# Attention maxima: one row block in eight found from a difference of scores

## The reference

```
keys = x @ jnp.triu(Wk).T
queries = x @ jnp.tril(Wq).T
values = x @ Wv.T
...
dot = jnp.einsum('bqhs,bkhs->bhqk', queries, keys) * scale
att = jax.nn.softmax(dot, axis=-1)
out = jnp.einsum('bhqk,bkhs->bqhs', att, values).reshape(b, t, e)
return out @ Wu.T + bu
```

## Time and profile before

| | us |
|---|---|
| median of 3 runs | 1860.84 |
| lowest and highest | 1859.8, 1864.69 |
| profiled execution, its own time | 1861.46 |
| its span, first to last instruction | 1859.7 |
| VectorE busy in the span | 1450.8 (78%) |
| TensorE busy | 1504.6 (81%) |
| ScalarE busy | 898.7 (48%) |
| GpSimd busy | 356.7 (19%) |
| mean granted TensorE clock | 0.914 |

### The profile page before, as it was taken

The page is one execution under the profiler, slowest core; times in us unless marked ns, Lnnn a source line. Parts: engine busy times, 40 slices in busy tenths (PEclk is TensorE's granted clock), DMA queues, the critical chain, the costliest instruction groups (busy, mean ns, idle before and its releaser), DMA issues. The chain is left out here.

```text
span 1859.7 us, 27986 instructions
## 1 busy us (share of the span) xinstructions
PE 1504.6 (81%) x8404; PEld 776.2 (42%) x8404; DVE 1450.8 (78%) x2457; ACT 898.7 (48%) x1698; POOL 356.7 (19%) x390
## 2 busy tenths in 40 slices
PE   3699998998989998599956566665999769886698
PEld 2011221221212211388842122222888558666586
DVE  5799998998989993565577999998655558579674
ACT  3068887887778888332227333333322332230221
POOL 4000000000000000000013666662000114323143
PEclk9589999999999999799979899988999879989699
DMA  7100010000000001000001222220000012200123
GB/s 262 48 2 22 24 36 25 22 22 22 22 23 22 28 17 47 7 1 1 0 0 26 68 63 62 73 62 12 1 1 0 1 47 71 68 1 1 46 68 94
DMA packets 39528, 65.92 MB, mean 35 GB/s; under 512 B 11471, under 2 KB 16287, under 8 KB 38680
## 3 DMA queue, kind: packets, MB, share of 16 engines
q1 hardware_dynamic: 39400, 64.29, 11.3%
HBM read 57.28 MB, written 6.88 MB: 35 GB/s over the span
## 5 line engine op out<-in xcount | busy, mean ns | idle before, releaser
L688 DVE TENSOR_REDUCE row_max<-ps 128x1 f32<-128x1024 f32 x512 | 602.0, 1220 | 59.9 <-PE ps L560 52.2
L636 ACT ACTIVATE probs<-ps 128x512 f32<-128x512 f32 x1024 | 529.6, 604 | 113.1 <-PE ps L573 112.8
L560 PE MATMUL ps<-k_stack,q_stack 48*128 48x512 bf16 x1024 | 326.6, 406 | 59.9 <-DMA k_stack<-k_parts_dram 21.4
L573 PE MATMUL ps<-q_stack,k_stack 51*128 51x512 bf16 x1024 | 341.4, 390 | 13.0 <-ACT probs L636 11.0
L590 PE MATMUL ps<-probs,v_head 128*16 128x512 f32 x2048 | 276.0, 606 | 0.5 <-issue 0.3
L560 PEld LDWEIGHTS ps<-k_stack,q_stack 48*128 48x128 bf16 x1024 | 72.6, 95 | 408.8 <-DVE row_max L688 358.1
L1137 PE MATMUL ps<-s_hc,ident 128*128 128x512 f32 x256 | 142.9, 645 | 98.9 <-DVE s_hc L1337 98.9
L1073 POOL TENSOR_TENSOR s_dbx<-s_dx_c,s_b_rows 128x512 f32<-128x512 f32 x128 | 163.7, 1302 | 96.8 <-DVE s_h L1328 59.1
L845 ACT ACTIVATE e_gate<-ps 128x512 f32<-128x512 f32 x128 | 76.1, 598 | 201.4 <-PE ps L220 196.2
L1328 DVE TENSOR_TENSOR_SCAN s_h<-ps,s_state,s_dbx 128x512 f32<-128x512 f32 x128 | 156.8, 1266 | 0.9 <-DVE x_res L1305 0.9
L874 DVE TENSOR_TENSOR e_hidden<-e_gate,ps 128x512 f32<-128x512 f32 x128 | 87.6, 687 | 60.1 <-ACT e_gate L845 51.5
(11 more groups left out here) (344 smaller groups left out, 1989.0 us busy)
## 6 DMA issues: line engine op xcount, KB each, us to landing
s_b_rows<-s_b_dram SPq DMA_DIRECT2D x64, 256.0 KB, 3.1
m_spread<-m_probs_dram SPq DMA_DIRECT2D x128, 128.0 KB, 3.0
q_stack<-q_parts_dram SPq DMA_DIRECT2D x32, 96.0 KB
k_stack<-k_parts_dram SPq DMA_DIRECT2D x32, 96.0 KB
w_w<-w_dram SPq DMA_DIRECT2D x1, 2048.0 KB, 8.5
q_stack<-q_parts_dram SPq DMA_DIRECT2D x32, 64.0 KB
k_stack<-k_parts_dram SPq DMA_DIRECT2D x32, 64.0 KB
o_dram<-o_sb SPq DMA_DIRECT2D x64, 32.0 KB
```

The costliest lines, as they stand in the source:

```text
L560: last = nc.tensor.matmul(core.ps[:, 2 * b + r, :], qst[buf][0:KROWS, u * P:(u + 1) * P], kst[buf][0:KROWS, key:key + CH], start=True, sto ...
L573: nc.tensor.matmul(core.ps[:, S_BANK + n % S_RING, :], kst[buf][HALF:ROWS, kt * P:(kt + 1) * P], qst[buf][HALF:ROWS, c * CH:(c + 1) * CH], ...
L636: nc.scalar.activation(probs[:, us % RING, c * CH:(c + 1) * CH], core.ps[:, S_BANK + n % S_RING, :], ACT.Exp).then_inc(exp_done, 1)
L688: nc.vector.tensor_reduce(mx[:, u, b:b + 1], core.ps[:, 2 * b:2 * b + 2, :], mybir.AxisListType.XY, ALU.max).then_inc(max_done, 1)
```

## The change

For every fourth query block of each head (`u % EVERY == AT`, with 4 and 3), the first half of its keys is handled in another way: that is one of eight maxima. Bank 0 gets the scores with the first 512 keys, as before. Into bank 1 go the scores with the second 512 keys and, added to them by a further matmul, the scores with the first 512 keys negated, so that the bank holds the difference. ScalarE writes the positive part of that difference into SBUF (`keep_above`). VectorE adds this to bank 0, which gives the larger of the two scores at each place, and takes the maximum over the 512 places in the same operation. Ahead of it VectorE sets a one-column tile, `ready`, which carries the waits. GpSimd writes the negated keys of each head (`negate_k`) once the head's stack has landed.

```
+        k_neg = [sb(f"k_negated{i}", [KROWS, CH], BF16) for i in range(NBUF)]
...
+            def negate_k(buf, turn):
+                pool.wait_ge(stacked[buf], turn * STACK + STACK)
+                nc.gpsimd.tensor_tensor(k_neg[buf][:], kst[buf][0:KROWS, 0:CH], by_minus[0:KROWS, :].to_broadcast([KROWS, CH]),
+                                        ALU.mult).then_inc(k_negated, 1)
...
                     pool.wait_ge(pv_done, j * BODY + (par + 1 - NBUF) * NT)
                     stage_v(j * NBUF + par, par)
+                    negate_k(par, j)
                     cut_max(j * NBUF + (par - 1))
...
+                    apart = u % EVERY == AT and b == 0 and r == 1
                     last = nc.tensor.matmul(core.ps[:, 2 * b + r, :], qst[buf][0:KROWS, u * P:(u + 1) * P],
-                                            kst[buf][0:KROWS, key:key + CH], start=True, stop=True)
+                                            kst[buf][0:KROWS, key:key + CH], start=True, stop=not apart)
+                    if apart:
+                        pe.wait_ge(k_negated, j * NBUF + (gs // NT + 1))
+                        last = nc.tensor.matmul(core.ps[:, 1, :], qst[buf][0:KROWS, u * P:(u + 1) * P],
+                                                k_neg[buf][:], start=False, stop=True)
...
+            def keep_above(j, gs):
+                act.wait_ge(p1_done, j * (2 * BODY) + (2 * gs + 1))
+                nc.scalar.activation(above[:], core.ps[:, 1, :], ACT.Relu).then_inc(above_done, 1)
...
+                    if c == 1 and (us + LAG_S) % EVERY == AT and (j is not LOOPED):
+                        keep_above(j, us + LAG_S)
...
+                        if u % EVERY == AT and b == 0:
+                            dve.wait_ge(above_done, head * (NT // EVERY) + (u // EVERY + 1))
+                            nc.vector.memset(ready[:], 0.0)
+                            nc.vector.tensor_tensor_reduce(out=larger[:], in0=core.ps[:, 0, :], in1=above[:], scale=1.0,
+                                                           scalar=LOWEST, op0=ALU.add, op1=ALU.max,
+                                                           accum_out=mx[:, u, 0:1]).then_inc(max_done, 1)
+                            continue
```

More of the change, by code:

```diff
@@ L27 @@
 EPS = 1e-5
+LOWEST = -3.4028235e38
 HEADS = 16
@@ L339, in softmax_attention @@
         o_sb = sb("o_sb", [P, CH])
+        EVERY, AT = 4, 3
+        k_neg = [sb(f"k_negated{i}", [KROWS, CH], BF16) for i in range(NBUF)]
+        by_minus = sb("by_minus", [P, 1])
+        ready = sb("ready", [P, 1])
+        above = sb("above_zero", [P, CH])
+        larger = sb("larger", [P, CH])
         whole = [probs[:, i, :] for i in range(2)]
@@ L361, in softmax_attention @@
         max_done = core.sem("a_max_done")
+        k_negated = core.sem("a_k_negated")
+        above_done = core.sem("a_above_zero")
         nm_found = core.sem("a_nm_found")
@@ L400, in _ @@
             sp.wait_ge(parts_stored, 16 * 2 * NPART)
-            sp.wait_ge(ones_set, NBUF + 2)
+            sp.wait_ge(ones_set, NBUF + 3)
             def load_stack(head, par):
@@ L472, in _ @@
             nc.gpsimd.memset(by_one[:], 1.0).then_inc(ones_set, 1)
+            nc.gpsimd.memset(by_minus[:], -1.0).then_inc(ones_set, 1)
             for par in range(NBUF):
@@ L480, in _ @@
             pool.wait_ge(proj_used, 2 * NC_ + NC_)
-            pool.wait_ge(ones_set, NBUF + 2)
+            pool.wait_ge(ones_set, NBUF + 3)
             def stage_v(head, par):
@@ L507, in _ @@
                 nc.gpsimd.memset(a[:], 1.0).then_inc(cleared, 1)
+            for buf in range(NBUF):
+                negate_k(buf, 0)
             for head in range(NBUF - 1):
@@ L517, in _ @@
             stage_v(HEADS - 1, (HEADS - 1) % NBUF)
+            negate_k((HEADS - 1) % NBUF, LOOPED)
             for head in range(HEADS - 2, HEADS):
@@ L645, in _ @@
             act.wait_ge(core.o_zeroed, 1)
+            for gs in range(AT, LAG_S, EVERY):
+                keep_above(0, gs)
             def body(j, units, first=False):
```

## The result

The changed kernel takes 1890.36 us (median of 4 runs, 1888.12 to 1893.66) against 1861.84 for the kernel before (4 runs): 28.5 us more, ratio 1.0156 with a 95% interval of 1.0136 to 1.0175. The forecast was 1904 with a range of 1884 to 1924: right in its direction and its mechanism, and half as large again as the loss, 42.8 us against 28.5.

What follows compares the result with a forecast made beforehand. VectorE and the loop through TensorE and ScalarE, both near 2.385 us a unit, were taken as the bound; 60 changed units x 0.65 plus 4 x 0.94 in the first head, 42.8 us, on 1861.46 give 1904 us, range 1884 to 1924.

Steps and rivals of the forecast that it cites:

- Two loops: Maxima stage: one loop through TensorE and ScalarE at 2.385 us a unit, VectorE alone at 2.345, 0.04 to spare.
- VectorE waits inside the unit: Changed unit: VectorE, free at t0+0.60, waits for ScalarE's positive part until t0+1.64, 1.04 us of new idle time.
- What VectorE does in place of the 1024 columns: VectorE, changed unit: memset, add-and-maximum and accumulator read take 0.90 us instead of 1.18, saving 0.28.
- The sum per unit: Changed unit: 1.04 idle less 0.28 saved is 0.76 us late; three units repay about 0.11, leaving 0.65.
- First head: First head, where no exponentials run and the clock is 0.50: 0.94 us later, four times, 3.8 us.
- GpSimd, and the matmul: GpSimd's key negation, below 1.3 us a head, and TensorE's added matmul, 0.38 us, both costed at nothing.
- ScalarE's place alone counts: Rival: VectorE's wait is repaid and only 0.27 to 0.29 us per changed unit stays, 1878 us; chance 0.08.
- The precedent of the copy: ScalarE's output copy, once a head between two units' exponentials, after which VectorE idles 0.29 us.
- VectorE is the bound and gains: Rival: VectorE never waits; 18 us saved, of which the TensorE and ScalarE loop allows 10, 1851 us; chance 0.04.
- rival 4: VectorE's add-and-maximum streams its two inputs at half rate, 2 x 0.69 us, 44 us more, 1948 us; chance 0.08.
- rival 5: ScalarE reloads tables between exponential and positive part and back, 2 x 1.283 x 64 = 164 us more; chance 0.02.
- The signs: Profile after: VectorE idle near 1.0 us each, about 64 in all; TensorE's waits grow equally; changed two-maximum period near 3.1.

Runs made afterwards that it cites:

- half dose: The changed kernel with two changed query blocks a head (every eighth) instead of four: 1874.7 us, ratio 1.0068 against the kernel before.
- the kernel without hand-over: The changed kernel with all added work, but positive part and add-and-maximum use constant tiles and VectorE doesn't wait for ScalarE: 1867.2 us, ratio 1.0032.
- the last experiment: The changed kernel with sixty one-column matmuls issued on TensorE ahead of the first head: 1886.3 us, ratio 1.0136 against the kernel before.

## Why the prediction was right in kind and too large

*What bounds the kernel before.* Two loops of nearly one period, with no room to repay. Right of the loop through ScalarE: shorter exponentials shorten the period, VectorE's shorter work doesn't (the runs with shorter exponentials and with VectorE's part alone). Wrong of VectorE: its 2.345 a unit, the mean of the first head, is not its own limit. Behind a changed unit its maxima start 1.136 and 1.131 us apart, 2.27 a unit, and with shorter exponentials the whole runs at 2.325.

*VectorE waits inside the unit.* Right in its place and nearly in its size: 0.95 us in the quiet unit against 1.04. The start of the positive part was forecast at t0+0.92 and measured at t0+0.93, its end at t0+1.52 both times. Too large was the step from ScalarE to VectorE: 0.04 us (424.20 to 424.24) and not 0.12 of the earlier trace rows.

*What VectorE does in place of the 1024 columns.* **This is the term that was mis-sized.** I added 0.69, 0.11 and 0.10 to 0.90; the three take 0.61 from start to start. The addition itself was right (0.686 against 0.687 in the earlier trace rows); wrong was to lay two small instructions end to end with it, when the earlier trace rows already showed maxima starting before the one ahead had ended. The memset was over-priced besides: the trace of before had one of a single column, 59 ns, that I had passed over for the one of 64 columns:

```profile
L2219 DVE MEMSET one<- 128x1 f32 x1 | 0.1, 59 | 0.9 <-PEq L2248 0.9
```

The saving is 1.18 - 0.61 = 0.57 and not 0.28. The rule of the Trainium skill ("VectorE: DVE Perf Modes", "The DRAIN you can't avoid") that the next operation waits for the pipeline to empty would give 0.83 with the measured durations, 0.22 more than the trace has. But the same section of the Trainium skill goes on that an operation which is not held starts earlier, which the prediction left out; with that the trace agrees, for the next maximum starts 0.61 behind an add-and-maximum of 0.686.

*The sum per unit.* 0.95 - 0.57 = 0.38 late, and 0.11 of it repaid: 0.27, against 0.65. The amount repaid is the one forecast, but by luck: not 0.04 in each of three units, but nearly all in the next two starts of maxima (medians of 1.136 us for 1.244 before, and 1.131 for 1.141), and nothing in the units after, since TensorE is late by then and its own loop has no room.

*First head.* Forecast 3.8 us more; with the smaller VectorE term the same working gives 0.94 - 0.29 - 0.08 = 0.57, 2.3 us for four; the first head's maxima took 2.8 us longer.

*The range.* That the measured time lies in it owes something to luck. With the VectorE term right and nothing else, the same working gives 0.36 per unit and 0.65 in the first head, 24 us and 1885, at the edge of the range of 1884 to 1924. With the step from ScalarE right too it gives 60 x 0.27 + 2.3 = 18.5 us and 1879, below the range. The overpriced terms stood in for some 9 us that the sum doesn't have.

*Not in the sum.* The changed units give 60 x 0.27 = 16 us and the first head some 3; the stage grew by 27.6. The other 9 us are mostly stalls of TensorE, which the prediction had put at nothing: at the 19th slot, for the maxima's transfer, and at the loop's edges. For the transfer TensorE's matmuls wait 4.7 us in the changed kernel, 0.3 at half dose and 0.2 in the kernel without hand-over, so this part needs both the number of changed units and their lateness, or comes from where these put the fetches; why, is open. The part at the edges goes with TensorE's code, as the idle times beside the last experiment show.

*GpSimd, and the matmul.* Hidden, as costed: the negation takes 1.03 us a head, and no wait for it stands in the list of waits. No table load came between exponential and positive part (L666 has a single one in the changed kernel, at 95.8 us): the Trainium skill's statement ("ScalarE: Activation LUTs", "Table sets: the hidden batching unit") that relu is in every set agrees with the trace, where the positive part costs 0.59 us and its neighbours start 0.49 apart.

*Rivals.* That ScalarE's place alone counts is refuted: 0.08 us per changed unit and 0.7 us in all. The precedent of the copy misled as a price: in the earlier trace rows the copy starts 0.10 us after the exponential ahead of it has ended, and the positive part 0.10 before (423.61 against 423.71). That the copy waits there for the values before it follows from the code and is not measured. That VectorE is the bound and gains is refuted by the run with its part alone. Half rate for the addition (rival 4) and a table load (rival 5) are refuted by the 0.686 and by the single load.

*The signs.* VectorE's idle time is as announced (0.95 in the quiet unit, 68.3 us for all 64) and the positive part starts 0.93 behind its unit. Three signs did not come: from the last maximum ahead of a changed unit to the unit's own second one it is 2.77 us and not 3.1, the three instructions 0.61 and not 0.9, and TensorE's matmuls wait for VectorE 29 us more (13.8, then 39.2 + 3.6) and not some 64. Each differs in the way of the mis-sized term.

## What to carry to other kernels

Where three engines run in step with nearly equal periods, look for the order in which they hand a tile on: a shorter operation on the busiest engine can be worth less than nothing if its new input comes from a third engine within the same step. The loss is the new idle time, less what the shorter operation saves and what the engine can repay before the others run late too: here 0.95 - 0.57 - 0.11. Place the extra hop on the part of a step that has other work ahead of it (here the second pair of banks: less than half of the loss). Time saved on a consumer that is fed through double buffers was not stored for later here.

Small instructions beside a long one on VectorE should be priced by start-to-start distances, not by their durations. And where one term is too large, ask what it may be hiding: here the range held because an overpriced term covered stalls that nobody had counted.

## What was not expected of the hardware

A memset of one column (59 ns), an add-and-maximum of 512 columns (686 ns) and an accumulator read (83 ns) without waits between them hold up VectorE's next maximum for 0.61 us, less than the longest of them. An added 0.59 us operation on ScalarE, between exponentials that start 0.49 us apart, cost the kernel 0.7 us for all 64 (interval of the ratio 0.9995 to 1.0015). From the end of the issue of four 3 KB stores to the load that waits for them it took 1.0 us in most heads, 1.6 in three of the kernel before, and 2.4 to 3.3 in three other heads of the kernel before and four of the changed one, in each of which a 16 KB instruction fetch ran near that time. Sixty small matmuls ahead of TensorE's loop changed its idle time at the loop's edges from 17.3 to 12.5 us.
